# Writing out the group loop of a code search on all engines, with constant wait counts

## What is computed

```python
# layer 0: a spectral convolution (cosine transform, low modes mixed over the channels, back)
x = x + _L0_conv_ref(_gn(x), L0_conv_weights1, L0_conv_weights2)
# layer 1: every 64 consecutive numbers are replaced by the nearest of 1024 code vectors
sim = jnp.einsum('nd,dk->nk', flat, embeddings)
codes = jnp.argmin(y_sq + e_sq - 2.0 * sim, axis=1)
quantized = jnp.take(embeddings.T, codes, axis=0)
x = x + quantized.reshape(input_shape)
```

## Time and profile before

| what | value |
|---|---|
| median of three runs | 7052.71 us (7044.49 to 7055.29) |
| profiled execution, span | 7063.4 us |
| TensorE matmul busy | 6410.4 us (91%) |
| VectorE busy | 6502.3 us (92%) |
| ScalarE busy | 4723.1 us (67%) |
| GpSimd busy | 4788.5 us (68%) |
| mean granted TensorE clock | 0.974 of full speed |

### The profile page before, as it was taken

The page is one execution under the profiler, slowest core; times in us unless marked ns, Lnnn a source line. Parts: engine busy times, 40 slices in busy tenths (PEclk is TensorE's granted clock), DMA queues, the critical chain, the costliest instruction groups (busy, mean ns, idle before and its releaser), DMA issues. The chain is left out here.

```text
span 7063.4 us, 142290 instructions
## 1 busy us (share of the span) xinstructions
PE 6410.4 (91%) x25616; PEld 2523.4 (36%) x25616; DVE 6502.3 (92%) x19053; ACT 4723.1 (67%) x12193; POOL 4788.5 (68%) x4614
## 2 busy tenths in 40 slices
PE   7998799999999999899999999999999999999997
PEld 3457333333333333333333333333333333333332
DVE  7781399999999999999999999999999999999998
ACT  2341477777767777677777777777777776777775
POOL 0000277777777777777777777777777777777777
PEclk9898799999999999999999999999999999999999
DMA  7999466665656656566666656666666665666665
GB/s 247 293 297 174 90 143 143 147 143 141 147 137 144 142 143 148 140 143 142 146 143 143 141 145 144 143 145 141 146 142 144 146 142 138 143 145 145 143 142 119
DMA packets 1138992, 1075.92 MB, mean 152 GB/s; under 512 B 702944, under 2 KB 843040, under 8 KB 1138144
## 3 DMA queue, kind: packets, MB, share of 16 engines
q1 hardware_dynamic: 924640, 651.61, 35.5%
q0 software_dynamic: 196608, 411.30, 27.1%
q10 hardware_dynamic: 16896, 4.20, 0.3%
HBM read 722.32 MB, written 143.01 MB: 123 GB/s over the span
## 5 line engine op out<-in xcount | busy, mean ns | idle before, releaser
L1040 POOL DMA_INDIRECT arena<-table,idx x4096 | 4030.6, 984 | 1448.1 <-issue 1170.8
L728 ACT ACTIVATE arena<-bank 128x512 f32<-128x512 f32 x4096 | 2433.8, 594 | 1470.1 <-PE bank L558 1288.1
L558 PE MATMUL bank<-eh,t 128*128 128x512 f16 x8192 | 2486.7, 385 | 491.8 <-DVE mx L935 273.7
L935 DVE CUSTOM_DVE_ANT_0 arena<-bank,arena 128x512 f32<-128x512 f32 x4096 | 2765.4, 675 | 52.3 <-ACT arena L728 50.4
L945 DVE FIND_INDEX8 idx<-mx,arena 128x8 uint32<-128x512 f32 x4096 | 2805.6, 685 | 0.0
L558 PE MATMUL bank<-el,t 67*128 67x512 f16 x8192 | 2472.4, 383 | 0.0
L558 PEld LDWEIGHTS bank<-eh,t 128*128 128x128 f16 x8192 | 578.9, 98 | 2446.5 <-issue 1329.2
L558 PEld LDWEIGHTS bank<-el,t 67*128 67x128 f16 x8192 | 810.6, 99 | 990.8 <-issue 33.9
L1047 POOL TENSOR_TENSOR X<-X,arena 128x1024 f32<-128x1024 f32 x256 | 605.5, 2365 | 11.2 <-DVE arena L970 5.0
L523 PE MATMUL conv<-iw,Ts 64*128 64x512 f32 x1024 | 582.4, 649 | 0.0
L537 PE MATMUL bank<-arena,ident 128*128 128x512 f32 x1024 | 545.1, 613 | 5.0 <-ACT arena L708 4.6
(11 more groups left out here) (107 smaller groups left out, 4570.1 us busy)
## 6 DMA issues: line engine op xcount, KB each, us to landing
X<-x SPq DMA_DIRECT2D x512, 512.0 KB, 4.6
y<-X SPq DMA_DIRECT2D x256, 512.0 KB, 4.4
t<-t SPq DMA_DIRECT2D x512, 128.0 KB
arena<-table,idx POOLq DMA_INDIRECT x4096
arena<-w SPq DMA_DIRECT2D x12, 2048.0 KB, 22.7
arena<-w SPq DMA_DIRECT2D x64, 128.0 KB, 3.0
t<-YS SPq DMA_TRANSPOSE x512
spec<-Fs SPq DMA_DIRECT2D x256, 16.0 KB, 3.8
```

Source lines behind the costliest of these rows:

```text
L558: last = nc.tensor.matmul(bank[4 + place(k) % 2 if e else k % 4][:], tile[0:rows, g.buf2, k], codes[0:rows, e], start=rows == P, stop=rows ...
L728: nc.scalar.activation(R[:, k % 4], bank[4 + place(k) % 2][:], ACT.Relu).then_inc(b_rl, 1)
L935: V.tensor_tensor_reduce(out=Fm[:, k % 4], in0=bank[k % 4][:], in1=R[:, k % 4], scale=1.0, scalar=-3.0e38, op0=ALU.add, op1=ALU.max, accum ...
L1040: G.indirect_dma_start(out=q[:, g.buf2, k], out_offset=None, in_=table, in_offset=bass.IndirectOffsetOnAxis(ap=idx[:, g.buf2, k, 0:1], axis=0)
```

## The change

On all five engines the loop and its five bodies per trip give way to 31 passes written out by Python. `i` is then always a Python integer: every count is a constant, `hold` adds nothing, and no register, compare or branch instruction is left in the third stage. What each engine computes, its order, the buffers and the waits stay. The diff for TensorE, with the constants that go:

```diff
-BODIES = 5
-assert (NI - 2) % BODIES == 0
...
             body_b(0)
-            with pe.Fori(0, (NI - 2) // BODIES) as i:
-                for n in range(BODIES):
-                    body_b(BODIES * i + n + 1)
-            body_b(NI - 1)
+            for i in range(1, NI):
+                body_b(i)
```

More of the change, by code:

```diff
@@ L396, in _ @@
             body(0)
-            with sp.Fori(0, (NI - 2) // BODIES) as i:
-                for n in range(BODIES):
-                    body(BODIES * i + n + 1)
-            body(NI - 1)
+            for i in range(1, NI):
+                body(i)
             for r in range(U - 2, U):
```

## The result

The changed kernel takes 7003.56 us in the median of four runs (7002.21 to 7007.16), the kernel before 7050.09 us in four runs: 46.5 us less. The ratio is 0.9938, with a 95% interval of 0.9924 to 0.9952, which is 34 to 54 us. The forecast was 40 us less and a range of 6985 to 7045 us; the time lies in the range and in the likeliest case.

A forecast was written before the change was run, and what follows sets the result against it. The prediction took GpSimd, issuing gathers, to set the pitch, with VectorE sometimes waiting. Jumps 26 us plus constants and holds 14 us made 40 us, taken from the median 7052.7 to give 7013 us; range 6985 to 7045.

The forecast's parts named there:

- the likeliest case: Whole kernel: both gains arrive, 7013 us, spanning 6990 to 7028 us; chance 0.77.
- The five jumps, 26 us: Third stage, trip ends: the five long intervals between GpSimd's finishing additions shrink to the ordinary pitch, saving 26 us.
- Constants and holds, 14 us: GpSimd between gathers: constants replace register counts and holds, saving 14 us over 240 looped groups, bounds 5 to 31.
- The two gaps: GpSimd ahead of gathers: after the addition 0.80 to 0.77 us; every fifth group's long one 1.65 to 1.50 us.
- The same instructions on the other engines, nothing: VectorE, TensorE, ScalarE, SyncE: dropping register counts and holds there gains nothing, as they still meet the same gather.
- The stops did not recur elsewhere: Rival on TensorE: stops come whatever the code and return elsewhere; 7039 to 7053 us, chance 0.11.
- VectorE did not become the bound: Rival: gathers issue quicker and groups take VectorE's own 23.62 us; about 6875 us, chance 0.05.
- Gathers did not collide more: Rival: one more gather per group falls under a VectorE product, 0.45 us each; 7121 us, chance 0.07.
- The Trainium skill's 108 ns for a branch: Jumps back: at this documented price six are worth 0.6 us, giving about 7038 us; forecast used the measured row instead.
- the row: Profile row at a trip's end: TensorE stops 4.44 us at a jump back, forty times the documented branch price.
- What was to be seen: Third stage signs: pitch near 24.2 us, ScalarE waits under 10 us, gathered-row waits above 80 us, gaps 0.77 and 1.50.
- The clock at 1.00 throughout: Third stage sign: the granted clock, 0.52 or 0.57 behind trip ends before, stays at 1.00.

The follow-up runs named there:

- e8: Changed kernel with each group's small power moved from GpSimd to ScalarE's reciprocal root function; 6883.67 us.
- e7: Changed kernel with one extra semaphore increment put back ahead of each of the 4096 gathers on GpSimd, no registers; 7020.67 us.
- e1: Kernel before with only TensorE's program written out, the other four engines keeping the loop; 7023.28 us against 7050.96.
- e3: Changed kernel with TensorE alone keeping its loop of six trips (five jumps back); 7024.01 us.
- e9: e8 with TensorE alone in the loop of six trips (five jumps back); 6922.00 us.
- e5: Changed kernel with TensorE alone in a loop of two trips of 15 passes, one jump back; 7007.48 us.
- e6: Changed kernel with TensorE alone in a loop of 30 trips of one pass, 29 jumps back; 7139.17 us.
- e2: Kernel before with only GpSimd's program written out, the other engines keeping the loop; 7030.06 us, ratio 0.9970.

## Why the prediction held, point by point

*What bounds the kernel.* GpSimd, and not VectorE with its 92%: shown by e8, where 0.47 us less of GpSimd's work per group made the group 0.488 us shorter, and borne out by e7, where instructions added on GpSimd alone made it 0.068 us longer. VectorE is close behind: e8 has only 0.05 us per group on top of VectorE's busy time.

*The five jumps, 26 us.* Measured 27.7 us (e1), 20.5 us (e3), and 26 us in the profile. Counting the loss on GpSimd instead of VectorE was right: e9 shows the larger price, some 6 us, where VectorE can make up little. That TensorE's loop is the cause, and the only one among five engines, is shown by e1 and e3; that it is the jump in it, by e5 and e6.

*Constants and holds, 14 us.* The sum came out too small here. The profiles give (24.253 - 24.142) x 240 = 27 us, inside the bounds of 5 to 31 but twice the value taken; the runs give 20.9 us (e2). The two gaps that made up the 14 us moved as read, from 0.80 to 0.78 and from 1.65 to 1.49 us, and with GpSimd alone written out the pitch inside the trips fell by (24.253 - 24.194) x 240 = 14 us, the value taken. What the sum had not is outside those gaps: in e2 the five long intervals were 7.9 us shorter in all, and in the changed kernel the gathers themselves were busy for 8.6 us less (4030.6 to 4022.0), which no term had. The pitch of pass 31, 24.125 us, was nearer to the outcome than the sum of single gaps.

*The same instructions on the other engines, nothing.* This is not shown. 48.6 us from e1 and e2, against 46.5 for all five engines, leave nothing for ScalarE, VectorE and SyncE; but e3, in which they are written out beside GpSimd, is 6.0 us faster than e2, with gathers that are busy for 8.9 us less. Each sum is uncertain by more than that, and the gathers' busy time also differs between e5 and e6 (4017.5 and 4040.4 us), where all four engines but TensorE have the same program. So the term is small, and whether it is zero stays open.

*The rivals.* The stops did not recur elsewhere: TensorE's longest wait is 1.1 us. VectorE did not become the bound: it still waits 103.7 us for gathered rows; e8 shows what that rival would have looked like, and its 23.62 us per group was close to the 23.654 reached there. Gathers did not collide more, as far as their busy time tells: it fell.

*The Trainium skill's 108 ns for a branch* would have given 7038 us. The runs decide for the row: 4 to 5 us per jump over long code in e3 and e6.

*What was to be seen.* A pitch near 24.2 with no interval over 26 us, no stop of TensorE above 3 us, gaps of 0.78 and 1.49 us, 8.0 us of waits for ScalarE and 103.7 us for gathered rows: as written, to within 0.01 us. The clock at 1.00 throughout was wrong for four stretches between 1960 and 6692 us.

*How much of it was luck.* The jumps came out within 6 us of their term, by the mechanism read from the rows. The second term had its size from two rows, and the runs put it at 14 to 27 us, depending on how it is taken. The 6.5 us between the total and the forecast lie within the interval of 34 to 54 us, so that the total comes this near says little about either term; e1 and e2 say more.

## What to carry to other kernels

Before pricing loop overhead, find the engine that sets the pitch by an instruction that runs once per iteration, and look at the gaps that no semaphore ends: an engine with 68% busy time can be the slowest. In these runs a jump back over long code stopped TensorE for 4 to 6 us and the granted clock fell behind it, so one jump cost less than could be told (e5), while 29 jumps cost 136 us (e6); where only a few programs can be written out, TensorE's is the first, then that of the engine at the bound. And such gains are small beside 0.47 us per group taken off the slowest engine, which was worth 120 us.

## What the runs showed of the hardware that was not expected

A semaphore increment ahead of each gather on GpSimd cost 3 to 4 ns on average (e7); 11.3 of the 17.1 us stand in idle time ahead of gathers, at the few places where the engine had to wait. Every fifth group one gather has a gap of some 1.5 us ahead of it whether counts are constants or not; its cause is open, but VectorE's longest waits for gathered rows, and the falls of the granted clock behind them, come mostly with it, and in e8, where GpSimd needs less time for a group, the clock stays at 1.00 from 1030 to 6850 us. Jumps back on ScalarE, VectorE, GpSimd and SyncE over 40 groups of code cost nothing that could be told in e1.
